# Four stages of a 4-layer decoder rewritten: third self attention by scores, slots and combine pipelined, TensorE adds the six shares

## Time and profile before

| | |
|---|---|
| median of 3 runs | 4386.25 us (4383.8 to 4393.79) |
| profiled execution, its time / its span | 4399.44 us / 4397.5 us |
| TensorE, VectorE, ScalarE, GpSimd busy | 74%, 65%, 41%, 16% of the span |
| mean granted TensorE clock | 0.817 of 2.4 GHz |

### The profile page before, as it was taken

One profiled execution on the slowest core, in us unless ns is written; L12 is line 12 of the kernel. 1 busy time (PEld: TensorE's weight loads), 2 busy tenths in 40 slices (PEclk: granted clock), 3 DMA queues, 4 the chain that ended last, 5 costly groups with the idle time before them and its releaser, 6 DMA issues. The chain is left out here.

```text
span 4397.5 us, 70729 instructions
## 1 busy us (share of the span) xinstructions
PE 3267.4 (74%) x22305; PEld 2394.5 (54%) x22369; DVE 2842.7 (65%) x8231; ACT 1802.4 (41%) x5188; POOL 681.8 (16%) x867
## 2 busy tenths in 40 slices
PE   3668379366654886755777876999899997786887
PEld 3546269222222664534454754666577775554777
DVE  6556633499995876174898263555467775556997
ACT  1346334111112664212777233222155553435886
POOL 0045533100002777200000120000100000000000
PEclk9789589666666665577788685999999998998999
DMA  4040168200004000420300011333200000000000
GB/s 116 1 166 0 33 195 234 73 0 0 0 0 154 3 0 1 126 95 18 74 0 0 1 38 34 103 100 99 86 1 0 0 0 4 0 0 15 1 0 19
DMA packets 135723, 196.88 MB, mean 45 GB/s; under 512 B 24858, under 2 KB 90840, under 8 KB 133846
## 3 DMA queue, kind: packets, MB, share of 16 engines
q1 hardware_dynamic: 124078, 186.31, 14.0%
q0 software_dynamic: 11520, 9.05, 0.7%
HBM read 151.49 MB, written 58.63 MB: 48 GB/s over the span
## 5 line engine op out<-in xcount | busy, mean ns | idle before, releaser
L1260 PE MATMUL l_attn_p_s<-l_attn_outer,l_attn_upper 128*128 128x512 f32 x256 | 204.5, 973 | 113.9 <-DVE l_attn_outer L1203 100.0
L95 POOL TENSOR_TENSOR rstd<-vareps,minus_half 128x32 f32<-128x32 f32 x11 | 59.9, 5444 | 1391.7 <-DVE vareps L86 1258.0
L2583 ACT ACTIVATE l_ffn_sg<-l_ffn_p_g 128x512 f32<-128x512 f32 x168 | 100.3, 597 | 355.4 <-PE l_ffn_p_g L2620 355.4
L2554 DVE TENSOR_TENSOR l_ffn_part<-l_ffn_sg,l_ffn_share 128x512 f32<-128x512 f32 x168 | 116.3, 693 | 190.8 <-ACT l_ffn_sg L2583 183.3
L2610 PEld LDWEIGHTS l_ffn_p_o<-l_ffn_wd,l_ffn_h 128*128 128x128 f32 x1344 | 175.7, 191 | 85.2 <-issue 76.1
L1418 POOL DMA_INDIRECT slots_in<-l_xattn_x,l_xattn_slot x192 | 190.3, 991 | 83.8 <-issue 49.9
L1260 PEld LDWEIGHTS l_attn_p_s<-l_attn_outer,l_attn_upper 128*128 128x128 f32 x256 | 79.2, 324 | 218.7 <-issue 174.4
L2730 ACT ACTIVATE l_attn_E<-l_attn_p_s,l_attn_nm 128x128 f32<-128x128 f32 x512 | 181.2, 386 | 2.9 <-DVE l_attn_nm L2688 2.9
L2610 PE MATMUL l_ffn_p_o<-l_ffn_wd,l_ffn_h 128*128 128x128 f32 x1344 | 178.1, 275 | 2.3 <-DVE l_ffn_h L2557 1.6
L2620 PE MATMUL l_ffn_p_g<-l_ffn_f_xTall,l_ffn_wg 128*128 (+1 forms) x336 | 173.7, 599 | 0.5 <-DVE l_ffn_turned L2545 0.5
L2622 PE MATMUL l_ffn_p_u<-l_ffn_f_xTall,l_ffn_wu 128*128 (+1 forms) x336 | 172.5, 595 | 0.0
(11 more groups left out here) (806 smaller groups left out, 9436.5 us busy)
## 6 DMA issues: line engine op xcount, KB each, us to landing
l_experts_w<-in_L_ffn_w SPq DMA_DIRECT2D x72, 512.0 KB
l_ffn_share<-share_rows SPq DMA_DIRECT2D x112, 256.0 KB, 3.2
slots_in<-l_xattn_empty SPq DMA_DIRECT2D x8, 2145.0 KB, 24.0
shares_out<-l_xattn_zero SPq DMA_DIRECT2D x24, 512.0 KB, 11.5
l_combine_got<-shares_out SPq DMA_DIRECT2D x16, 768.0 KB, 4.5
l_attn_toep<-kernel_rows SPq DMA_DIRECT2D x1, 8192.0 KB, 31.1
xattn_toep<-ssm_rows SPq DMA_DIRECT2D x1, 8192.0 KB
l_slots_w<-in_L_ffn_w SPq DMA_DIRECT2D x32, 176.0 KB
```

The costliest lines, as they stand in the source:

```text
L1260: mm = pe.matmul(p_s[:, r, a], upper[:], outer[:, r, a * 512:(a + 1) * 512], start=True, stop=True)
L2554: dve.tensor_tensor(part[:, w], sg[:, w], share[:, slot], ALU.mult).then_inc(s.share_used, 1)
L2583: act.activation(sg[:, k], p_g[:, k], ACT.Silu).then_inc(s.silu_ready, 1)
```

## The change

Four stages change.

1. `l1_attn` forms no states. `scored` gives, for each sequence, the products of every token's key with every other token's key (and then query) in all 16 heads, in 32-row tiles, from kTm, four copies of the keys with all but one head's rows of each 32 zeroed. VectorE multiplies the key scores by the causal triangle out of PSUM; for the query scores ScalarE copies PSUM to SBUF and GpSimd multiplies by the triangle. `applied` then multiplies each head's 128x128 block by that head's 8 columns of the gradient on TensorE. k and q are projected turned, apart from the other three. The pipeline is 4 deep, and one more weight is loaded.
2. `l1_slots` takes single steps in a pipeline 2 deep (three products of three steps), with four buffers for input and weights, all written out; it starts without semaphores counted up ahead.
3. `l1_combine` and `l2_attn` become `l1_out`: 16 pairs, 4 deep. TensorE adds the six shares by products with the identity into the PSUM tile of the shared expert's down product. The norm's statistics, power and shift are formed per pair, xhat on ScalarE, the bias added by GpSimd.
4. `l3_xattn`: `out` and kT go behind the shift products, `out` gets its own place in PSUM, and VectorE's parts are reordered with them.

The core of the diff:

```diff
 def l1_attn
+            def _(pool):
+                    for b, u in item(1):
+                        for r in range(2):
+                            pool.wait_ge(s.scores2_read, b * 2 + (r + 1))
+                            pool.tensor_tensor(queries[:, u % 2, r], queries[:, u % 2, r], causal, ALU.mult).then_inc(s.queries_ready, 1)
             def _(dve):
-                def applied(psum, b, read, part, x, step):
-                    for r in range(2):
-                        dve.wait_ge(psum, b * 2 + (r + 1))
-                        dve.tensor_tensor(square(part[:, r]), square(p_s[:, r].rearrange("p a n -> p (a n)")),
-                                          over_columns(x[:, r * P:(r + 1) * P]), ALU.mult).then_inc(read, 1)
-                    dve.wait_ge(read, b * 2 + 2)
-                    chain(dve.tensor_reduce(step, part[:].rearrange("p r (m i) -> p (r m) i", i=HD), AX.X, ALU.add))
...
-                        for r in range(2):
-                            dve.tensor_tensor(square(outer1[:, r]), over_columns(k_[u][:, r * P:(r + 1) * P]),
-                                              over_rows(dz1[:, r * P:(r + 1) * P]), ALU.mult).then_inc(s.outer1_ready, 1)
+                    for b, u in item(0):
+                        for r in range(2):
+                            dve.wait_ge(s.scores1_psum, b * 2 + (r + 1))
+                            dve.tensor_tensor(keys[:, r], scores, causal, ALU.mult).then_inc(s.keys_ready, 1)
             def _(act):
+                def copied(b, u, r):
+                    act.wait_ge(s.scores2_psum, b * 2 + (r + 1))
+                    act.activation(queries[:, u % 2, r], scores, ACT.Copy).then_inc(s.scores2_read, 1)
...
+                        for m in range(SUB):
+                            last = act.activation(kTm[:, u % 2, :, m], side(p_y[:, 0:W]), ACT.Identity, scale=head4[:, m:m + 1], bias=bhead[:, m:m + 1])
             def _(pe):
-                def states(b, r, ready, psum, outer):
-                    pe.wait_ge(ready, b * 2 + (r + 1))
-                    for a in range(2):
-                        mm = pe.matmul(p_s[:, r, a], upper[:], outer[:, r, a * 512:(a + 1) * 512], start=True, stop=True)
+                def scored(u, r, c):
+                    for m in range(SUB):
+                        for j in range(4):
+                            rows = slice(32 * j, 32 * j + 32)
+                            mm = pe.matmul(p_s[:, j, m * P:(m + 1) * P], kTm[rows, u % 2, r, m], kq[rows, u % 2, c, r * P:(r + 1) * P], start=True, stop=True)
+                def applied(out, a, r, dz):
+                    for h in range(H):
+                        mm = pe.matmul(out[:, r * P + h * HD:r * P + (h + 1) * HD], a[:, h], dz[:, r * P + h * HD:r * P + (h + 1) * HD], start=True, stop=True)
...
+  order on TensorE, by lag: mean(3), transposes(0), scored q r0 (1), kq(0), ctxT(4), squares(3), scored q r1 (1), out(4),
+  projections(0), applied key r0 and r1 (1), scored k r0 (0), applied query r0 (2), scored k r1 (0), applied query r1 (2)

 def l1_slots (TensorE)
-                with pe.Fori(0, NP // W) as i:
-                    for u in range(W):
+                for item in written_out(2, NP, V):
+                    for n, u in item(0):
+                        pe.wait_ge(x_in[u], (n // V + 1) * DMA)
+                        after(pe, s.xT_ready, n - 1)
+                        pe.transpose(p_x[:, n % 2, 0:P], x[:, u, 0:D], R.ident[:]).then_inc(s.xT_psum, 1)

-def l1_combine(nc, R, A, ys, xTall):
-                            summed = dve.tensor_reduce(total[:, r], got[:, v * 2 + r].rearrange("p r (k d) -> p r d k", k=K), AX.X, ALU.add)
-def l2_attn(nc, R, A):
+def l1_out(nc, R, A, ys, xTall):
+                    for b, u in item(1):
+                        after(pe, s.x_added, b)
+                        pe.wait_ge(got_in[u], (b // V + 1) * DMA)
+                        for n in range(K):
+                            pe.matmul(p_d[:, 0:W], R.ident[:], got[:, u, :, n], start=(n == 0), stop=False, skip_group_check=True)
+                        pe.wait_ge(s.h_ready, b + 1)
+                        for r in range(2):
+                            for f in range(FC):
+                                mm = pe.matmul(p_d[:, r * P:(r + 1) * P], h[:, u % 2, f, r * P:(r + 1) * P], wd[:, f * P:(f + 1) * P],
+                                               start=False, stop=(f == FC - 1), skip_group_check=True)
+  order on TensorE, by lag: gate and up(0), memory and sums(3), transposes(2), shares and down(1), memW(3), kv and q(2), out(3)

 def l3_xattn (TensorE)
-                    for b, u in item(4):
-                        pe.matmul(p_r[:, 0], headsT[:], wo[:], start=True, stop=True).then_inc(s.out_psum, 1)
                     for b, u in item(2):
                         pe.wait_ge(s.shift_spread, b + 1)
-                    for b, u in item(1):
-                        pe.matmul(p_c[:, 0:SC], wkv[:, 0:P], cT[:, u % 2], start=True, stop=True).then_inc(s.kT_psum, 1)
-                    for b, u in item(2):
                         for m in range(SUB):
...
                         mm.then_inc(s.shifted_psum, 1)
+                    for b, u in item(4):
+                        pe.matmul(p_c[:, 256:384], headsT[:], wo[:], start=True, stop=True).then_inc(s.out_psum, 1)
+                    for b, u in item(1):
+                        pe.matmul(p_c[:, 0:SC], wkv[:, 0:P], cT[:, u % 2], start=True, stop=True).then_inc(s.kT_psum, 1)
```

More of the change, by code:

```diff
@@ L1075, in wide @@
             return t.unsqueeze(2).broadcast_to((P, 2 * H, HD))
[L1077 to L1086, removed]
+        causal = upper[:].unsqueeze(1).broadcast_to((P, H, P))
+        scores = p_s[:].rearrange("p j (m t) -> p (j m) t", m=SUB)
         with nc.Block() as block:
@@ L1180, in _ @@
-                    for b, u in item(3):
+                        dve.wait_ge(s.step1_psum, b * 2 + 2)
+                        dve.tensor_tensor(z2[:], z[u], p_z[:, 0:W], ALU.subtract).then_inc(s.z2_ready, 1)
+                    for b, u in item(3):
+                        dve.wait_ge(s.mean_psum, b + 1)
+                        chain(dve.tensor_scalar(st3[:, 0], p_w[:, W:W + 2 * H], 1.0 / (HD * S), None, ALU.mult))
+                        dve.tensor_tensor(heads(qw[u]), heads(qw[u]), wide(st3[:, 0]), ALU.subtract).then_inc(s.centred_ready, 1)
@@ new lines, in _ @@
+                    for b, u in item(2):
+                        dve.wait_ge(s.sq2_ready, b + 1)
+                        dve.tensor_reduce(st2[:, 0], heads(t2[:]), AX.X, ALU.add).then_inc(s.var2_ready, 1)
+                    for b, u in item(3):
+                        dve.wait_ge(s.sq3_ready, b + 1)
+                        dve.tensor_reduce(gs[:, 1], heads(t3[:]), AX.X, ALU.add).then_inc(s.squares_ready, 1)
+                    for b, u in item(1):
+                        dve.wait_ge(s.std1_ready, b + 1)
+                        gradient(z[u], vg[u], n1[:], d1[:], t1[:], st1)
+                        dve.tensor_tensor(heads(dz1[:, u % 2]), heads(d1[:]), wide(st1[:, 1]), ALU.mult).then_inc(s.dz1_ready, 1)
@@ L1293, in _ @@
                         mm.then_inc(s.ctxT_psum, 1)
+                    for b, u in item(3):
+                        pe.wait_ge(s.squares_ready, b + 1)
+                        pe.matmul(p_w[:, W + 2 * H:W + 4 * H], R.ones[:], gs[:, 1], start=True, stop=True).then_inc(s.sqmean_psum, 1)
                     for b, u in item(1):
-                        for r in range(2):
-                            after(pe, s.part2_read, b * 2 + (r - 1))
-                            states(b, r, s.outer1_ready, s.states1_psum, outer1)
+                        pe.wait_ge(s.scores2_read, b * 2 + 1)
+                        scored(u, 1, 1).then_inc(s.scores2_psum, 1)
@@ new lines, in _ @@
+                    for b, u in item(1):
+                        pe.wait_ge(s.dz1_ready, b + 1)
+                        for c, _ in item(4):
+                            pe.wait_ge(s.out_taken, c + 1)
+                        for r in range(2):
+                            applied(p_z, keys[:, r], r, dz1[:, u % 2]).then_inc(s.step1_psum, 1)
+                    for b, u in item(0):
+                        for c, _ in item(1):
+                            pe.wait_ge(s.scores2_read, c * 2 + 2)
+                        scored(u, 0, 0).then_inc(s.scores1_psum, 1)
@@ L1304, in _ @@
[L1304 to L1311 removed]
+                        pe.wait_ge(s.keys_ready, b * 2 + 1)
```

609 lines of the change are left out of this document (303 added, 306 removed).

## The result

The changed kernel takes 4594.52 us (median of 4 runs, 4584.89 to 4602.69), the kernel before 4386.69 us on the same chip: 1.047 times as long, 95% interval 1.0446 to 1.0495. The forecast was 4451 us with a range up to 4560; the sign was right, the size was not. The profiled execution took 4592.69 us, its span is 4590.9.

A forecast was written before the change was run, and what follows sets the result against it. No engine bounds the whole program before; TensorE becomes the third self attention's bound. +149 there, -54 joined stage, -10 slots, -20 last cross attention make +65 us on 4386: 4451 us, range 4330 to 4560.

The forecast's parts named there:

- The waits term: Third self attention: TensorE's own waits, for mean and out, of 2 us a pair at the low clock, 4 high.
- The division by the mean clock: Third self attention: 22.2 us of TensorE work a pair at the high level, divided by mean clock 0.58.
- Prologue, fill and drain I keep: Third self attention: the stage's ends stay as before; the fifth stage of the skew adds fill but no work.
- Rival 2: Third self attention: GpSimd's masks block VectorE and delay dz1, up to 5 us a pair, +80, 4531 us; chance 0.14.
- The doubt that the trace before had no run of thin products starting high: Third self attention: the forecast fails above all if thin products do not lower an already high clock; no size given.
- The rule of the Trainium skill: Third self attention: keeping TensorE continuously busy brings the full clock, making a pair 26 us and the whole kernel faster.
- Rival 1: Third self attention: the clock holds through the thin products, 26 us a pair at 1.00, kernel 4227 us; chance 0.12.
- 3 (0.50 flat): Third self attention: waits keep the clock from rising in the dense part, 46 us a pair, kernel 4547 us; chance 0.12.
- 4 (joined stage low): Joined combine and attention: its clock stays low too, +79 in place of -54, kernel 4584 us; chance 0.06.
- the 19: Joined stage: 19 us for a slow start, fill and drain of four more items, within its 168 us.
- VectorE's 43.7 us of reductions: Joined stage: VectorE loses 16 reductions of 2.77 us, 43.7 us, in a stage forecast to gain 54 us.
- the -10: Slots: 11 us without TensorE go if no wait remains, ScalarE's order keeps a little, so -10 us.

The follow-up runs named there:

- The experiment: The changed kernel with l1_attn's query masks made by VectorE straight from PSUM instead of by GpSimd: 4537.6 us, 1.0342 times the time before.
- the four kernels above: Changed kernel 4594.52 us; with query masks on VectorE 4537.6; with applied products streaming 128 columns 4400.89; with both 4341.62.
- the shares' experiment: Changed kernel with the old l1_attn (4296.34 us), but VectorE instead of TensorE adds the six shares in the joined stage: 4292.86 us.

## Why the prediction was wrong

**Step by step, the self attention.** The forecast for a pair was 22.2 us of work / 0.58 + 2 us of waits = 40. Measured in the window 1102.2 to 1150.8: mean clock 0.58, as chosen; TensorE busy 41.6 us, where 22.2 / 0.58 gives 38.3; waits 7.0, where "I take 2 us low" stood. So:

- *The waits term failed*, by 5 us a pair. The two waits that it named are as sized, `mean` 0.96 and cT 1.17 us, 2.1 together. It lacked the 4.29 us ahead of the keys' thin products (1.36 with the masks on VectorE) and ScalarE's projection copy, 0.58.
- *The division by the mean clock failed*, by 2.5 us a pair. It takes for granted that TensorE works through the high spell as through the low one. It works in 3.8 of the 7.6 us at the high level and in 37.8 us at the low one, which is 3.8 + 37.8 / 2 = 22.7 us of work. The work was sized well, 0.5 above the sum (0.8 at this clock); the mean of 0.58 came true, but half of what was high in it went into waits. The masks' wait thus costs twice: it takes the end of the high spell, and the thin group behind it has none (13.79 against 11.91 us). The experiment puts the masks at 4.1 us a pair in all, 66 us in the stage (828.0 to 761.7).
- *"Prologue, fill and drain I keep"* failed: 828.0 - 16 x 48.6 = 50 us against 34.

16 x (48.6 - 30.7) = 286, and 17 for the edges, make the 303 us. Of the 154 above the forecast, 66 are the masks, 71 are what else a pair takes above 40 us (16 x some 4.5: with the masks on VectorE it takes 44.5, TensorE busy 40.0 and waits 4.5), 17 the edges.

**The cases were laid out as alternatives.** Rival 2, that the masks block VectorE, had its mechanism, place and price right (+80 for 66), but only a chance of 0.14, as if it excluded the rest. Nothing in it depends on the clock: the four kernels above, with and without either edit, show both effects whole beside each other. The row with which I argued, an add that took 0.982 us for 0.426, was misread as a single case. The timeline of before has three of the sixteen adds longer (0.83, 0.98 and 0.98 us), and each began just after an L2300 of GpSimd. Two of them, GpSimd's instruction first:

```profile
2495.21 0.73 POOL L2300 TENSOR_TENSOR x<-x,xattn_bo 128x256 f32<-128x256 f32 x1 [4.09 <-ACT l_mix_xh L2370]
2495.24 0.98 DVE L2346 TENSOR_TENSOR l_mix_xt<-l_mix_xt,l_mix_xh 128x256 f32<-128x256 f32 x1 [3.13 <-ACT l_mix_xh L2370]
2506.83 0.72 POOL L2300 TENSOR_TENSOR x<-x,xattn_bo 128x256 f32<-128x256 f32 x1 [3.74 <-ACT l_mix_xh L2370]
2506.85 0.98 DVE L2346 TENSOR_TENSOR l_mix_xt<-l_mix_xt,l_mix_xh 128x256 f32<-128x256 f32 x1 [1.68 <-ACT l_mix_xh L2370]
```

With two masks of 4.5 us in every pair such a meeting was likely, and the open question was where they fall. The sum should have had them, and 4531 been the middle; even that is 63 us short of the 4594.5 measured.

**What was right.** Which engine would bound the pair, the work it has, the price of thin products at either level, and, in part by luck, the mean clock. The doubt that the trace before had no run of thin products starting high is settled: the clock falls within the first 32 of them. The rule of the Trainium skill that the prediction weighed (TensorE: Matmul & The Clock Gate, Why this matters for your kernels), busy without gaps brings the full clock, does not hold here: from 1109.86 to 1141.5 us TensorE runs 32 us without a gap, all of it at the low level. Rival 1 (clock holds), 3 (0.50 flat) and 4 (joined stage low) are refuted by clocks of 0.58 and 0.96; that rival 4's 4584 us lies next to the time measured is chance.

**The other parts.** The joined stage: 138 us of TensorE, 11 of loads and 19 of slow start and fill were forecast; its window shows 139.7 busy and 13.6 idle, so the 19 were not there. That VectorE's 43.7 us of reductions had to go was beside the point, as the shares' experiment shows. The slots' step went from 2.38 us to 2.17 in the timeline, 7 us for 32 steps, and the second input now comes 1.8 us late at the start: -5, where nearly all of the 11 us without TensorE had been counted as waits that go, -10. (The 16 loads of 2.42 us are those of two steps, so they are 1.21 of a step's 2.6 us and not over half; the -10 does not rest on it.) The cross attention gave 26 to 28 for 20.

## What to carry to other kernels

Ask of a stage bound by weight loads at which clock it will run, and whether the engine works or waits while the clock is high. Here zero-padding the moving side of thin f32 products from 8 to 128 columns, 16 times the arithmetic with the same weight loads, took 13 us off a pair of 49. When a wide elementwise step goes to GpSimd, look which two-input step of VectorE meets it, charge that step the whole duration (here 4.5 us, twice a pair), in the sum and not as a rival, and look whether the engine that waits behind loses its clock too. Test the named part of a rewrite by itself: the joined stage was just as fast without it.

## What the runs showed that was not expected

- With 64 moving columns two pairs side by side took 30.7 and 44.0 us, with granted clocks of 0.91 and 0.64, in one execution; with 8 and 32 columns (masks on VectorE) every pair took 39 to 46.5 us once the pipeline was full.
- Moving the sum of six shares from TensorE to VectorE changed its stage by under 1 us, with 21 us less of the one and 49 more of the other.
- What is left open: why the stage's ends cost 61 us with the wide products against 50 with the thin ones and 34 before. No run took the pipeline's depth apart.
